# A two-layer adaptive-norm transformer kernel on one core: the opening put into the searched order, one layer's modulation at a time, and new orders for everything

## What is computed

```python
x = L0_attn_x                                              # 16 x 256 x 128
mod = (silu(L0_c) @ L0_wmod).reshape(16, 6, 1, 128)        # sa, ca, ga, sb, cb, gb
ga, gb = sign(g) * maximum(abs(g), 0.25)                   # for g in ga, gb
h = layernorm(x) * (1 + ca) + sa
x = x + ga * attention(h)      # rmsnorm, q/k/v, rotary factor, causal softmax, 16 heads of 8, w_o
h = layernorm(x) * (1 + cb) + sb
x = x + gb * moe(h)            # top 2 of 8 experts 128-512-128 plus a shared expert, then max-normalised
mod = (silu(L1_c) @ L1_wmod) ...                           # the same six vectors for layer 1
h = layernorm(x) * (1 + ca) + sa
x = x + ga * scan_mixer_and_gated_ffn(h)
h = layernorm(x) * (1 + cb) + sb
x = x + gb * token_shift_ffn(h)
```

## Time and profile before

| | us |
|---|---|
| median of 3 runs (lowest, highest) | 750.18 (750.1, 751.65) |
| the profiled execution: its own time | 748.82 |
| the profiled execution: span of its instructions | 747.2 |
| PE busy, share of the span | 673.8, 90% |
| DVE busy | 502.8, 67% |
| ACT busy | 488.0, 65% |
| POOL busy | 401.1, 54% |
| mean granted TensorE clock | 0.976 |

### The profile page before, as it was taken

How to read it: one execution, slowest core, us unless ns; L and a number is a source line. 1 busy time by engine, 2 the same in 40 slices (tenths; PEclk the granted TensorE clock), 3 DMA queues, 4 the chain that set the end, 5 groups by cost and what they waited for, 6 DMA issues and landing times.

```text
span 747.2 us, 12574 instructions
## 1 busy us (share of the span) xinstructions
PE 673.8 (90%) x3615; PEld 430.0 (58%) x3615; DVE 502.8 (67%) x1894; ACT 488.0 (65%) x750; POOL 401.1 (54%) x571
## 2 busy tenths in 40 slices
PE   3899999989899989895999989986989999999994
PEld 3444544544455444444888889974656575556642
DVE  3498879997998899982354244412354869897663
ACT  1768687676787676574444445551588888888653
POOL 7327455384878595753214154425565776745443
PEclk9999999999999999996999999998999999999998
DMA  9993000000000000018667758841001101100002
GB/s 270 381 382 100 1 1 0 8 16 8 22 14 22 15 16 22 19 34 227 181 188 240 215 173 248 239 143 36 27 27 33 28 22 29 32 11 2 14 15 70
DMA packets 65631, 66.01 MB, mean 88 GB/s; under 512 B 7121, under 2 KB 48554, under 8 KB 65562
## 3 DMA queue, kind: packets, MB, share of 16 engines
q1 hardware_dynamic: 59296, 52.12, 23.0%
q0 software_dynamic: 6208, 13.07, 5.4%
q10 hardware_dynamic: 58, 0.02, 0.0%
HBM read 37.33 MB, written 27.85 MB: 87 GB/s over the span
## 4 chain that ended last, share of the span: by engine, by line
PE 43%; DVE 23%; issue 11%; ACT 7%; SPq 7%; POOL 5%; DMA 3%; POOLq 0%; DVEq 0%; another core or an unknown queue 0%; ACTq 0%
DVE JK L1325 8%; PE PS L1122 5%; PE PS L1102 4%; PE PS L984 3%; PE PS L1022 3%; PE PS L1198 3%; PE PS L927 2%; PE PS L933 2%; POOL got L2026 2%; DVE XN L1610 2%; PE PS L1024 2%; DMA got<-expert_rows,IU 1%; SPq L2111 1%; SPq L2109 1%; PE PS L939 1%
## 5 line engine op out<-in xcount | busy, mean ns | idle before, releaser
L1325 DVE CUSTOM_DVE_ANT_0 JK<-PS,CM 128x256 bf16<-128x256 f32 (+1 forms) x512 | 148.6, 351 | 8.0 <-PE PS L984 7.2
L1845 ACT ACTIVATE GF<-PS,XN 128x256 f32<-128x256 f32 (+1 forms) x156 | 70.3, 456 | 67.6 <-PE PS L1102 36.1
L984 PE MATMUL PS<-KZ,QS 128*128 128x512 f32 x192 | 87.9, 489 | 7.8 <-DVE MX L1325 4.7
L1122 PE MATMUL PS<-WD,GF 128*128 128x128 f32 x568 | 87.7, 275 | 0.0
L2026 POOL DMA_INDIRECT got<-expert_rows,IU x64 | 64.1, 1002 | 39.7 <-DMA got<-expert_rows,IU 22.4
L1122 PEld LDWEIGHTS PS<-WD,GF 128*128 128x128 f32 x568 | 79.8, 191 | 3.2 <-ACT WL L1852 0.3
L1998 POOL DMA_INDIRECT expert_rows<-five,IU x64 | 63.8, 996 | 33.0 <-DMA expert_rows<-five,IU 17.9
L1806 ACT ACTIVATE PA<-PS 128x1024 f32<-128x1024 f32 x64 | 63.9, 1024 | 13.1 <-PE PS L1007 10.4
L2011 POOL DMA_DIRECT2D expert_rows<-YT x39 | 21.4, 550 | 85.9 <-issue 65.3
L1987 POOL TENSOR_SCALAR_AFFINE_SELECT PA<-PA 128x256 f32<-128x256 f32 x128 | 50.6, 425 | 30.3 <-ACT PA L1806 30.0
L984 PEld LDWEIGHTS PS<-KZ,QS 128*128 128x128 f32 x192 | 34.8, 189 | 50.1 <-DVE MX L1325 21.5
(11 more groups left out here) (326 smaller groups left out, 1729.0 us busy)
## 6 DMA issues: line engine op xcount, KB each, us to landing
expert_rows<-five SPq DMA_DIRECT2D x16, 1024.0 KB, 12.8
WU<-in_L_ffn_up_w SPq DMA_DIRECT2D x39, 256.0 KB
WD<-in_L_ffn_down_w SPq DMA_DIRECT2D x39, 256.0 KB
XT<-expert_rows SPq DMA_DIRECT2D x32, 128.0 KB
expert_rows<-YT POOLq DMA_DIRECT2D x32, 128.0 KB, 3.3
BD<-in_L_ffn_down_b SPq DMA_DIRECT2D x39, 64.0 KB
PA<-in_L_attn_x SPq DMA_DIRECT2D x8, 256.0 KB, 5.7
out<-yo SPq DMA_DIRECT2D x8, 256.0 KB, 2.3
```

Source lines behind the costliest of these rows:

```text
L984: pe.matmul(bk.rearrange("p (j n) -> p j n", n=wd), q, ks, start=True, stop=True).then_inc(sems["mx_mm"], 1)
L1122: m = pe.matmul(bk[:, b], g[:, b], wd[:, k, :], start=(k == 0 and t == 0), stop=(k == 3 and t == blocks - 1))
L1325: m = dve.tensor_tensor_reduce(JK[n % 2][:, s], bk[:, s], CM[:, 256 - wd:256] if wd == 128 else CM[:, 0:256], -1.0, 3.0e38, ALU.add, ALU.m ...
L1845: act.activation(GF[slot["gf", kind, u, k]][:, 0:n], bank("up", kind, u, k)[:, 0:n], ACT.Gelu, bias=bias).then_inc(sems["gelu"], 1)
```

## The change

- `silu` is split into `cond` (ACT) and `silu` (DVE), `silu_t` into `silu_t` and `silu_c`, `modmm` into `modmm` (PE), `modc` (the copy and the two additions of 1) and `modg` (the gates), `vecs` into `vecs` and `vecc`. All are steps of the searched order, a job for each layer.
- `ln_mod` waits for its own layer's `modc` only; the attention's residual waits for layer 0's gates only.
- `wq` moves from POOL to DVE; the clearing of MP, which stood behind it on POOL, goes ahead.
- SP issues layer 0's conditioning first, and layer 1's behind the two modulation weights.
- The planner's costs: `load_late` holds SP 5.0 instead of 3.0 and lands 3.9 later, `fetch` 3.2 instead of 2.9; a step does not pay a hop to a step on its own engine; the three maxima of a group may be ordered apart; arrival times of the loads are written out; layer 1's jobs may begin at 4.5, not 3.0.
- `wsh`/`wsl` of tile 17 are put behind `ev` of tile 15 instead of behind all of the table's steps.
- `ORDER1` (1798 steps, now 1813) and `ORDER2` (707) are searched again.

```diff
-    "silu": ("ACT", 0.3, "exp"), "silu_t": ("PE", 0.3, None), "modmm": ("PE", 1.9, None), "vecs": ("PE", 0.3, None),
-    "ldt": ("PE", 0.436, None), "ldx": ("ACT", 0.478, None), "wq": ("POOL", 7, None),
+    "cond": ("ACT", 0.28, "exp"), "silu": ("DVE", 1.62, None), "silu_t": ("PE", 0.2, None), "silu_c": ("DVE", 0.17, None),
+    "wmod": ("DMA", 0.0, None), "modmm": ("PE", 1.2, None), "modc": ("DVE", 0.66, None), "modg": ("DVE", 1.4, None),
+    "vecs": ("PE", 0.2, None), "vecc": ("DVE", 0.6, None),
+    "ldt": ("PE", 0.436, None), "ldx": ("ACT", 0.478, None), "wq": ("DVE", 3.2, None),
...
-    "plan_rows": ("DVE", 4.9, None), "fetch": ("SP", 2.9, None), "load_late": ("SP", 3.0, None), "tw": ("PE", 0.4, None),
+    "plan_rows": ("DVE", 4.9, None), "fetch": ("SP", 3.2, None), "load_late": ("SP", 5.0, None), "tw": ("PE", 0.4, None),
...
-LANDS = {"fetch": 3.0, "store": 2.0}
+LANDS = {"wmod": 0.0, "fetch": 3.0, "store": 2.0, "load_late": 3.9}
...
-        yield stage("ln_mod", c, s, after=[("modmm", 1)])
+        yield stage("ln_mod", c, s, after=[("modc", int(s in ("a1", "f1")))])
...
-    for l in range(2):
-        put("silu", l)
-    for l in range(2):
-        take(RR, "silu_t", l, end=("silu_T", l))
-        put("silu_t", l)
-    jobs = [(1.0 + 1.5 * c, first(c)) for c in range(2)] + [(2.0, modulation(0)), (5.0, modulation(1)), (8.0, vectors()), (4.0, weights())]
+    arrives = (6.3, 7.4, 11.0, 11.7, 13.6, 14.4, 15.1, 15.9)
+    jobs = [(arrives[c], first(c)) for c in range(2)] + [(3.7, modulation(0)), (9.0, modulation(1)), (12.5, vectors()), (5.3, weights())]
...
-    weights_in(N1)
+    weights_in(N1, ("ev", "t", N1 - 2))
...
+        def wq():
+            w.wait_ge(ld_const, 16)
+            one = ident.rearrange("p (g j d) -> p g j d", g=4, j=4)
+            for a, ks in ((PH, (0, 1)), (PL, (2,))):
+                for k in range(4):
+                    dve.tensor_scalar(a[:, :, :, 8 * k:8 * k + 8], one, 1.0 if k in ks else 0.0, None, ALU.mult)
...
             w.wait_ge(*at("normed", c, s))
-            w.wait_ge(*at("mod", 1))
+            w.wait_ge(*at("mod_s", l))
...
+        sp.dma_start(cin[:, 0, :], i["L0_c"]).then_inc(ld_c[0], 16)
         sp.dma_start(CT[:, :], i["const"]).then_inc(ld_const, 16)
         sp.dma_start(xin[:, 0], xd[0]).then_inc(ld_x[0], 16)
-        for l in range(2):
-            sp.dma_start(cin[:, l, :], i[f"L{l}_c"]).then_inc(ld_c, 16)
```

More of the change, by code:

```diff
@@ L269, in arrange @@
         begun = free.get(engine, 0.0)
-        start = max([x[0], begun] + [done[(s, *k)] + hop for s, *k in after])
+        start = max([x[0], begun] + [done[(s, *k)] + hop for s, *k in after if cost(s, k)[0] != engine])
         for m, (ring, *_) in enumerate(takes):
-            start = max(start, ring.frees(done)[sum(r is ring for r, *_ in takes[:m])][0] + hop)
+            k = ring.frees(done)[sum(r is ring for r, *_ in takes[:m])][2]
+            ends = [(SIGNALS.get(s, s), wkey) for s, *wkey in ring.ends.get(k, ())]
+            start = max([start] + [done[(s, *wkey)] + hop for s, wkey in ends if cost(s, wkey)[0] != engine])
         waited = start > begun
@@ L346, in rmsnorm @@
         yield stage("rms_rs", c, s, takes=[(RS_, "rrs", (c, s), ("xn" if s == "q" else "xl", c, s))])
-        yield stage("rms_norm", c, s, after=[("vecs",)])
+        yield stage("rms_norm", c, s, after=[("vecc",)])
         if s != "q":
@@ L358, in modulation, with modulation_weights @@
     def modulation(l):
-        yield stage("modmm", l, takes=[(RR, "modmm", (l,), ("mod_cp", l))], after=[("modmm", l - 1)] if l else [])
+        yield stage("cond", l)
+        yield stage("silu", l)
+        yield stage("silu_t", l, takes=[(RR, "silu_t", (l,), ("silu_T", l))])
+        yield stage("silu_c", l)
+        yield stage("modmm", l, takes=[(RR, "modmm", (l,), ("mod_cp", l))], after=[("wmod", l)])
+        yield stage("modc", l)
+        yield stage("modg", l)
+    def modulation_weights(l):
+        yield stage("wmod", l)
     def vectors():
         yield stage("vecs", takes=[(RR, "vecs", (), ("vec",))])
+        yield stage("vecc")
     def weights():
@@ L390, in keys, with maxima @@
         yield stage(name, b, after=[("spe", b // 2, 4)] + ([("atm", b - 2, u) for u in range(6)] if b > 1 else []))
-    def maxima(b, g):
-        for u in range(3):
-            yield stage("mxm", b, g, u, takes=[(RR, "mx", (b, g, u), ("mx_red", b, g, u))],
-                        after=[("kzp", b), ("kza", b), ("spe", b // 2, g)] + ([("mh", b - 2)] if b > 1 else []))
-            yield stage("mxr", b, g, u)
+    def maxima(b, g, u):
+        yield stage("mxm", b, g, u, takes=[(RR, "mx", (b, g, u), ("mx_red", b, g, u))],
+                    after=[("kzp", b), ("kza", b), ("spe", b // 2, g)] + ([("mh", b - 2)] if b > 1 else []))
+        yield stage("mxr", b, g, u)
     def highest(b):
-        yield stage("mh", b, after=[("mxr", b, g, 2) for g in range(4)] + ([("qmt", b - 1, h) for h in range(2)] if b else []))
+        yield stage("mh", b, after=[("mxr", b, g, u) for g in range(4) for u in range(3)] + ([("qmt", b - 1, h) for h in range(2)] if b else []))
     def shifted(b, h):
@@ L543, in rows_in, with weights_in @@
         put("xs", t)
-    def weights_in(t):
+    def weights_in(t, ahead=()):
         if t >= NP:
@@ L550, in weights_in @@
         put("wsl", t)
-    weights_in(N1)
+        if ahead:
+            two = P.steps[-2:]
+            del P.steps[-2:]
+            at = P.steps.index(ahead) + 1
+            P.steps[at:at] = two
+    weights_in(N1, ("ev", "t", N1 - 2))
     rows_in(N1)
```

145 lines of the change are left out of this document (73 added, 72 removed).

## The result

The changed kernel takes 721.59 us (median of 4 runs, 719.34 to 722.81) against 750.38 (4 runs, 750.1 to 751.65): a ratio of 0.961, 95% interval 0.9583 to 0.9636. The forecast was 729. The profiled execution took 721.2 us, with a span of 719.6.

What follows compares the result with a forecast made beforehand. TensorE, busy 673.8 of 747.2 us, was taken as the bound. From 748.82 us, opening -5, attention 0, late weights -10, tile 17 +0.5 and join -6.5 gave 727.8; expected median 729, range 724 to 734.

Steps and rivals of the forecast that it cites:

- Opening: Start up to attention's first maxima: 5 us gained, maxima at 34 instead of 39.2; bounds 3 and 7.
- it waited for POOL, ends at 8.8 as before: Opening, silu's first DVE operation: held by POOL's memset of VA, so earlier conditioning brings nothing; other reading 1.6 us.
- Attention: Attention stage, new order throughout: taken as 0, with 5 us to either side; 20 us at the very best.
- the prediction's own sign: First maxima to last residual: prediction wrong if attention takes over 5 us more or less than before.
- Attention's order is better: Rival, attention stage: new order gives 5 or more of its 20 us, total 722; chance 0.12.
- the join's 6.5 us: Hole ahead of `fin2` 0: three quarters of 8.7 us of PE's time gained; bounds 2 and 9.
- my bound: Attention stage: busy times of PE and DVE in 294 us let it give back 20 us at the very best.
- Late weights: Behind attention: `tw` 0's 5.83 us wait and 4.9 us of slow clock go; 10 us taken, bounds 0 and 11.
- Tile 17: Ahead of tile 17: hole no smaller because of `plan_rows` on DVE, 0.5 us lost; bounds -0.5 and +1.
- Join and layer 1: From `fin2` 0 on: seven pieces fill 6.0 us of the 7.02 us hole and keep the clock up; 6.5 us gained.
- a rival at 0.12: Layer 1 gives the join's gain back: chain through gather, sum and norms is the bound; total 735, chance 0.12.
- Pieces done here are missing as filling later: Join: caution that pieces moved ahead of `fin2` 0 no longer fill layer 1's holes; 8.7 us cut to 6.5.

Runs made afterwards that it cites:

- e: Changed kernel with `wq`'s 16 selection-matrix operations back on POOL instead of DVE: 721.69 us, ratio 0.9617.
- f: Changed kernel with every `ln_mod` waiting for layer 1's modulation too, as in the kernel before: 723.88 us, ratio 0.9648.
- b: Kernel before with only `tw` 0 and its DVE step moved behind `up t 0 2`, right ahead of `tw` 1: 743.99 us, ratio 0.9912.
- d: Changed kernel with the attention steps in the former order, opening and tail kept new: 733.55 us, ratio 0.9774.
- a1: Changed kernel with `tw` 0 and its DVE step back ahead of the first shared down piece, `load_late` at its former cost: 728.01 us, ratio 0.9697.
- g: Changed kernel with `plan_rows` moved on DVE from ahead of `xs` 17 to behind `ev` 20: 718.53 us, ratio 0.9569.
- a2: Changed kernel with `tw` 0 back ahead of the shared down pieces, new `load_late` cost kept so fills go into the wait: 727.49 us, ratio 0.9689.
- c: Changed kernel with the former `ORDER2` for the last stages: 720.83 us, ratio 0.9599.
- j: Changed kernel with both `plan_rows` behind `ev` 20 and the former `ORDER2`: 716.1 us, ratio 0.9544.
- i: Changed kernel fetching only the first of each token's two expert rows and using it twice: 710.72 us, ratio 0.9472.

## Why the prediction was right in its direction and where it missed

**Opening: the gain was there, 2.9 us larger than forecast, and not by the step that I named.** The transpose at 8.65 (forecast 9.2), the first `ln_mod` at 15.57 (17.1), the first rms variance at 19.42 (21), the first maxima at 31.38 (34). Of the two readings of silu's first operation I took "it waited for POOL, ends at 8.8 as before". That step was wrong. It ended at 4.96, while POOL's memset of VA still stood at 7.87: the conditioning had landed earlier, and the operation was over before the memset began. The wait didn't go away; it moved to `wq`, which ran at 6.17. Its four operations on PH are one row above, from 6.17 to 8.99. What one line's instructions took (ns: least, median, most; then the first and last start) shows their spread:

```profile
L1303 DVE TENSOR_SCALAR PH<-CT x4: 491/1348/2201, 6.2 to 6.9; 128x128 fp32r<-128x128 f32 x4
L1303 DVE TENSOR_SCALAR PL<-CT x4: 202/652/1160, 8.9 to 10.2; 128x128 fp32r<-128x128 f32 x4
```

The longest took 2.20 us, the shortest 0.20. The last of PH ends at 8.99, 0.15 us behind the memset (7.87 + 0.97 = 8.84). The contention that I cited (the Trainium skill, "GPSIMD Engine Reference", "Key points") fits these ends. It fits the starts less well: the last of PH started by 6.9, before POOL's first memset on record (7.37), and at 0.20 us it would have been over by then. Which of the page's two conditions holds for these operations no run shows. My error was the moment, because I took the old time of the end for a fixed one although the operation now started 1.7 us earlier. It cost little: `wq` took DVE 4.9 us (6.17 to 11.10, forecast 3.8), the copy that the modulation needs was done at 11.53, and e shows no price of it that can be measured. f shows that what I named as the gain, one layer at a time, is about 2 of the 7.9 us. And some of the 7.9 is chance, as b's 2.9 us for the same opening show.

**Attention: the step that failed.** I wrote that I find "no row that says it does or doesn't, and take 0". It gave 8.4, and d puts the order's own worth at 8.4 to 10.8. By the prediction's own sign it is wrong here: attention took over 5 us less than before. This was one of the rivals at 0.12 ("Attention's order is better"), and its condition holds in full. Its 722 is the time that came, but by luck: it kept the join's 6.5 us, which didn't arrive. Nor was my bound sound: I took the 20 us of holes as the most that could come back. The holes fell by only 1.6 (20.0 to 18.4); PE's busy time fell by 6.9, 273.3 to 266.4, for 1,570 and 1,571 matmuls of nearly the same kinds (over the exact stretches 39.23 to 332.54 and 31.38 to 316.27; the changed kernel even makes one `ldt` and one `spm` more here, and three fills fewer). Of the 6.9, 4.3 stand in the score-maxima products alone (87.9 us busy before, 83.6 now, for 192 products each). Both stages have one stretch of low clock of the same length, so the clock isn't the reason. Matmuls' ends are modelled and overlap, so part of what counts as busy may have been waiting inside or between matmuls; that is an argument, not shown. Nor is it shown which pairs of steps did it: from one block's residual to the next, the new order takes up to 13.9 us less and up to 10.4 more, so no one place stands out.

**Late weights: right, the size 3.7 us short.** `tw` 0 waits for nothing, the clock is 1.00 through the stretch, and `xt` 1 waits 0.15 us (forecast 0.5):

```profile
331.12 0.49 PE L1157 MATMUL PS<-CT,gates 128*128 128x128 f32 x3
331.76 0.44 PE L1105 MATMUL PS<-CT,XT 128*128 128x128 f32 x2 [0.15 <-DMA XT<-expert_rows]
```

The stretch gave 13.7. I added 5.83 of wait and 4.9 of slow clock. a1 and b say that the wait and what follows it are worth 6 to 8 when they alone are moved: b's 7.7 and a1's 7.2 in this stretch. In b a short cold stretch stayed behind, and the tail that came back in a1 was half as long as the old one. So the price of 10.7 was too high for the step alone, and the other 6 of the 13.7 came with whatever else differs behind attention, which I hadn't counted. The rule I weighed, that a DMA wait is followed by a cold start (the Trainium skill, "TensorE: Matmul & The Clock Gate", section "HAM oscillation"), agrees with the traces here: 0.50 behind 5.83, 5.99 and 3.73 us of waiting for a DMA. How long the clock stayed low past the wait differed, about 11 us in the kernel before and 5 in a1, for waits of one length. What PE did in between differed too: in the kernel before it stood still once more, for 0.96 us before 348.73, and in a1 it was busy throughout from 330. Whether that is the reason isn't shown.

**Tile 17: right.** A hole of 3.80 (forecast about 4), released by DVE, +0.2 against +0.5, the clock down behind it. g shows the reason, `plan_rows` in that place, and what it costs: 2.7 to 3.1 us.

**Join and layer 1: the second term that failed, a rival at 0.12.** "Pieces done here are missing as filling later" was my caution, and I took three quarters of the gain all the same; nothing of it arrived. Two things. First, the seven pieces do fill 6.0 us of the hole, but POOL started the gathers 2.05 us later relative to the last product (it waited 4.22 for a store to land instead of 2.18), so the hole went from 7.02 to 2.96, over the 2 that I gave as a sign: 7.02 - 6.0 + 2.05 = 3.07. The first gather in the changed kernel, on POOL's timeline:

```profile
477.52 1.02 POOL L2047 DMA_INDIRECT got<-expert_rows,IU  x1 [4.22 <-DMA expert_rows<-YT]
```

From the end of the last product to the first gather it took 4.24 us in the kernel before, b, a2 and d, and 5.7 to 6.3 in the changed kernel and the seven others; why, stays open. And 2.96 us was still enough for the clock to fall to 0.50 (window 494 to 496 above). Second, `fin2` 0 hangs on the first gather by 15.87 us before and after, and `fin2` 1 and 2 on the later ones. PE has less filling now and waits at them instead: holes of 2.52 and 1.42 us where the kernel before had 0.30 and none, with a low clock behind the first of them too (0.57 in 514 to 518). The seven pieces stand behind the first gather in both orders, so a window from the first gather to the end has nearly the same work in both (823 and 816 matmuls), and the same holes, 23.0 and 23.1 us (the kernel before first):

```profile
505.52:747.19 241.67, 218.71 (x823) 132.28 (x822) 155.14 (x279) 174.22 (x242) 136.82 (x144) 0.97 0.10 27
477.52:719.57 242.05, 218.98 (x816) 131.26 (x814) 156.21 (x279) 166.14 (x235) 138.47 (x144) 0.98 0.10 27
```

The filling moved the holes and took none away. c and j show the same from the other side: with the 7 us hole back they are no slower. i shows that the gathers are a bound here: with half of them the hole at `fin2` 0 goes and the rest is 9.2 us shorter. They aren't the only one, since the holes at `fin2` 1 and 2 stayed. The 93% busy that I set against this rival is a mean over 217 us and said nothing about the first 50.

**Sum.** In span, the terms gave 2.9, 8.4, 3.7 and 0.3 us more than forecast, 15.3 together, and the join and the wait ahead of the gathers 6.9 and 1.8 less, 8.7 together. The 6.6 us between them is the miss, on a gain of 27.6. That the miss is no larger than this is luck: two terms of 8 and 7 us were wrong with opposite signs. Of the signs named beforehand, those on `tw`, the clock behind attention, `xt` 1 and tile 17 came true; chunk 0's transpose and the first maxima came earlier than 9 to 10 and 33 to 36, the hole ahead of `fin2` 0 was over 2 us, and attention is outside its 5 us.

## What to carry to other kernels

Price a stage that waits for transfers by the chain through them, from the transfer's issue to the step that wants it, and not by the filling one can put into the hole: filling taken from later comes back as a hole there. PE's holes are no upper bound on what a new order of many short matmuls can give: here its busy time fell by more than the holes did; a term without a row is an unknown with both ends, and here the unknown was worth 8 us, the largest single error of the forecast. A wait with a cold clock behind it is best closed by moving useful work into it: covering a part of it with fills bought nothing.

## What the runs showed that I had not expected

- Attention in the changed kernel still has a hole of 3.03 us, PE waiting for DVE's mask, with a low clock behind it; PE's timeline and a window:

```profile
290.40 0.19 PE L1094 MATMUL PS<-MASK,BEFORE 128*128 128x40 bf16 x1 [3.03 <-DVE MASK L1432]
292.00:296.00 4.00, 4.00 (x27) 2.48 (x20) 3.08 (x19) 0.60 (x1) 0.98 (x1) 0.57 0.02 4
```

- The clock fell to 0.50 behind empty stretches of 5.99, 3.73 and 2.96 us alike, and not behind one of 1.09; but in b it was at 0.63 in 344 to 348 with no wait over 0.76 us just ahead, where PE had been busy 3.14 of 4 us.
- Behind waits of nearly the same length (5.83, 5.99) it stayed low for about 11 us past the wait in one kernel and about 5 in the other.
- The same DVE operation on 128 columns took 0.20 us with POOL idle and 2.20 us in the stretch in which POOL's memsets of 512 and 1024 columns ran; silu's first operation took 0.22 with POOL issuing DMAs beside it, and 2.35 beside a memset.
